# A relational graph network on one core: row fetches shared out over three engines, loops written out, weights kept

## What is computed

```python
def _rgcn_layer(x, src, dst, edge_type, W, W_root, b):
    out = x @ W_root + b
    x_src = x[src]
    for r in range(R):                       # R = 8
        mask = (edge_type == r).astype(x.dtype)
        agg = segment_sum(x_src * mask[:, None], dst, n)
        cnt = segment_sum(mask, dst, n)
        out = out + (agg / maximum(cnt, 1.0)[:, None]) @ W[r]
    return out

for i in range(3):
    h = _rgcn_layer(h, src, dst, edge_type, Ws[i], W_roots[i], bs[i])
    if i < 2: h = relu(h)
return layernorm(x + h)
```

## Time and profile before

| | us |
|---|---|
| device time, median of 3 runs | 3286.82 (3285.97 to 3287.74) |
| span of the profiled execution | 4636.9 |
| GpSimd busy in the span | 2366.0 |
| TensorE busy in the span | 2709.5 |
| VectorE busy in the span | 1593.4 |
| ScalarE busy in the span | 785.7 |

### The profile page before, as it was taken

One profiled execution on the slowest core, in us unless ns is written; L12 is line 12 of the kernel. 1 busy time (PEld: TensorE's weight loads), 2 busy tenths in 40 slices (PEclk: granted clock), 3 DMA queues, 4 the chain that ended last, 5 costly groups with the idle time before them and its releaser, 6 DMA issues. The chain is left out here.

```text
span 4636.9 us, 70372 instructions
## 1 busy us (share of the span) xinstructions
PE 2709.5 (58%) x16749; PEld 2382.2 (51%) x16750; DVE 1593.4 (34%) x7090; ACT 785.7 (17%) x1465; POOL 2366.0 (51%) x2511
## 2 busy tenths in 40 slices
PE   2676655656566723565666666661466566566567
PEld 1665545555555613555555555560455455555557
DVE  1343333333333512333333333360233333333336
ACT  1021111111111211111111111130111111111114
POOL 6125555555555064555555555507455555555540
PEclk5566677666667856767666666685666676766669
DMA  3001111111111021111111111113111111111110
GB/s 89 14 17 42 38 39 41 38 39 41 38 39 41 5 77 35 40 40 39 40 39 39 40 39 39 41 28 85 33 40 41 38 38 41 39 38 41 39 36 29
DMA packets 109300, 185.02 MB, mean 40 GB/s; under 512 B 41145, under 2 KB 66054, under 8 KB 109062
## 3 DMA queue, kind: packets, MB, share of 16 engines
q0 software_dynamic: 79872, 163.74, 13.5%
q1 hardware_dynamic: 29190, 19.05, 1.5%
HBM read 173.02 MB, written 9.60 MB: 39 GB/s over the span
## 5 line engine op out<-in xcount | busy, mean ns | idle before, releaser
L354 POOL DMA_INDIRECT ring<-node_table,idx x1664 | 1575.1, 947 | 1410.6 <-POOLq L229 969.9
L1018 PE MATMUL ps_o<-sums,w_rel 128*128 128x128 f32 x4992 | 1036.4, 393 | 501.6 <-PEq L229 501.6
L1008 PE MATMUL ps_a<-onehot,ring 128*128 128x128 f32 x4992 | 948.2, 350 | 558.3 <-PEq L229 290.1
L1018 PEld LDWEIGHTS ps_o<-sums,w_rel 128*128 128x128 f32 x4992 | 979.7, 301 | 552.6 <-issue 552.5
L354 POOL DMA_INDIRECT ring<-in_x,idx x832 | 788.5, 948 | 726.7 <-POOLq L229 509.4
L1008 PEld LDWEIGHTS ps_a<-onehot,ring 128*128 128x128 f32 x4992 | 821.2, 250 | 587.1 <-issue 580.9
L561 DVE TENSOR_SCALAR onehot<-iota,key,weight 128x128 f32<-128x128 f32 x2496 | 867.5, 360 | 309.4 <-issue 280.6
L786 ACT CAST oh_cell_t<-ps_r 64x512 bf16<-64x512 f32 x645 | 372.8, 578 | 1735.2 <-ACTq L229 1660.5
L797 ACT COPY sums<-ps_a 128x512 f32<-128x512 f32 x624 | 365.2, 585 | 1667.6 <-ACTq L229 1649.8
L451 DVE TENSOR_TENSOR oh_cell<-cell_t,iota_bf 128x256 bf16<-128x256 bf16 x663 | 194.4, 294 | 1272.0 <-DVEq L229 655.8
L987 PE MATMUL ps_w<-inv_parts,oh_cell_t 64*128 x2652 | 264.9, 173 | 487.3 <-issue 291.8
(11 more groups left out here) (144 smaller groups left out, 638.1 us busy)
## 6 DMA issues: line engine op xcount, KB each, us to landing
ring<-node_table,idx POOLq DMA_INDIRECT x1664
ring<-in_x,idx POOLq DMA_INDIRECT x832
node_table<-ring SPq DMA_DIRECT2D x24, 256.0 KB
out_rows<-ring SPq DMA_DIRECT2D x12, 256.0 KB
w_rel<-in_L_gnn_Ws SPq DMA_DIRECT2D x3, 512.0 KB
raw_dst<-in_dst SPq DMA_DIRECT2D x1, 384.0 KB
raw_src<-in_src SPq DMA_DIRECT2D x1, 384.0 KB
raw_typ<-in_edge_type SPq DMA_DIRECT2D x1, 384.0 KB
```

What stands on the lines that cost most here:

```text
L354: nc.gpsimd.indirect_dma_start(out=ring[:, q, t, :], out_offset=None, in_=source, in_offset=bass.IndirectOffsetOnAxis(ap=idx[:, q, t:t + 1 ...
L1008: ins = nc.tensor.matmul(ps_a[b][:, t * KEYS:(t + 1) * KEYS], ring[:, q, t, :], onehot[:, b, t, :], start=True, stop=True)
L1018: ins = nc.tensor.matmul(ps_o[b][:, 0:PAIR * WIN], w_rel[:, r, :], sums[:, b, r, :, :].rearrange("p t w -> p (t w)"), start=(r == 0), stop ...
```

## The change

- **Fetching.** 75 of the 2496 tiles are no longer fetched by GpSimd. SyncE fetches 15 tiles in each layer, the fourth of their quads: quads 2, 14, 27, 40, 53, 66, 79, 92, 104, 117, 130, 143, 156, 169, 182. ScalarE fetches 8 tiles in layer one (quads 26, 50, 75, 100, 125, 150, 175, 200) and 11 in the others (26, 43, 60, 78, 95, 113, 130, 147, 165, 182, 200), the third of their quads. Such a tile takes 128 DMAs of one row each, whose address comes from a register; a register load brings eight node numbers at a time. SyncE works through a tile in one go. ScalarE issues eight rows behind each quad's work, over 16 quads, starting 25 quads ahead. `sum_edges` waits on their semaphores too.
- **Weights.** They are looked up in layer one only (`look`), kept in `weight` by a maximum (`keep_weights`), and used again in layers two and three.
- **Loops.** All 208 quads of a layer are written out; columns have fixed addresses. `idx` and `refill` are gone: GpSimd reads node numbers from `src_t`, and ScalarE gives slots free (`ring_free`) in `evacuate`.
- **Start.** GpSimd waits for the number of passes before its first gather; that number is made earlier, ahead of `bkt_i` on VectorE. The staging tiles `f_*` no longer lie in the ring.

```diff
-NL = NT // (G * GT)
+NQ = NT // GT
+FREES = G // 2
+LOADS = 8
+SYNC_TILES = 15
+ACT_TILES = (8, 11)
...
 NPAD = N + WIN
+GROUPS = [-AHEAD + lo - LOOKS[3] for lo in LOOKS[3:-1]]
+GROUPS += [q for n in range(NQ // G + 1) for q in (n * G + lo for lo in LOOKS[:-1])]
+STARTS = [q + AHEAD for q in GROUPS if q + AHEAD < NQ]
+def spread(first, last, n):
+    return [first + (last - first) * k // max(n - 1, 1) for k in range(n)]
+def owners(kind):
+    sync = {q * GT + GT - 1: "sync" for q in spread(2, NQ - G, SYNC_TILES)}
+    act = {q * GT + GT - 2: "act" for q in spread(26, NQ - 8, ACT_TILES[kind])}
+    return {**sync, **act}
+OWNERS = [owners(kind) for kind in range(2)]
...
         picked = sb("picked", [P, G * GT, NEAR, PARTS], F32)
...
+            def row_numbers(tile, b):
+                sp.reg_add(idx_of[b], idx_of[b], 16)
+                sp.dma_start(row_idx[0:1, b, :], src[tile * P:(tile + 1) * P].rearrange("(o e) -> o e", o=1))\
+                  .then_inc(sync_idx_in[b], 16)
+            def gather_rows(source, kind):
+                tiles = [i for i in range(NT) if OWNERS[kind].get(i) == "sync"]
+                with sp.Fori(0, count_of):
+                    take(sp, sync_pass_open)
+                    row_numbers(tiles[0], 0)
+                    for n, tile in enumerate(tiles):
+                        b, q, t = n % 2, tile // GT % G, tile % GT
+                        if n + 1 < len(tiles):
+                            row_numbers(tiles[n + 1], (n + 1) % 2)
+                        rows_before, idx_now = sp.snap(rows_of[b]), sp.snap(idx_of[b])
+                        sp.reg_add(rows_of[b], rows_of[b], P * 16)
+                        if n >= 2:
+                            sp.wait_ge(sync_rows_in[b], rows_before)
+                        sp.wait_ge(sync_idx_in[b], idx_now)
+                        sp.sem_inc(sync_step, 1)
+                        take(sp, sync_step)
+                        if tile >= G * GT:
+                            take(sp, sync_slot_free)
+                        for e in range(0, P, LOADS):
+                            node = load_value(sp, row_idx[0:1, b, e:e + LOADS], 0, N - 1,
+                                              "the graph's edges join its nodes")
+                            for j in range(LOADS):
+                                sp.dma_start(ring[e + j:e + j + 1, q, t, :], source[bass.ds(node[j], 1), :])\
+                                  .then_inc(sync_rows_in[b], 16)
+                    rows_now = [sp.snap(reg) for reg in rows_of]
+                    for b in range(2):
+                        sp.wait_ge(sync_rows_in[b], rows_now[b])
+                    sp.sem_inc(sync_step, 1)
+                    take(sp, sync_step)
             load_weights(0, 48)
...
+                sp.sem_inc(table_ready_act, 1)
                 take(sp, w_used)
                 load_weights(layer, layer * 48 + 48)
+                gather_rows(table, 1)
             take(sp, h_free)
...
-
-                    take(pool, idx_full[q])
+            def gather(source, kind):
+                for q in range(NQ):
+                    take(pool, ring_free[q % FREES])
                     for t in range(GT):
+                        if q * GT + t in OWNERS[kind]:
+                            continue
                         nc.gpsimd.indirect_dma_start(
-                            out=ring[:, q, t, :], out_offset=None, in_=source,
-                            in_offset=bass.IndirectOffsetOnAxis(ap=idx[:, q, t:t + 1], axis=0))\
...
-                          .then_inc(gathered[q], 16)
-
-            gather_ring(x)
+                            out=ring[:, q % G, t, :], out_offset=None, in_=source,
+                            in_offset=bass.IndirectOffsetOnAxis(ap=src_t[:, q * GT + t:q * GT + t + 1], axis=0))\
+                          .then_inc(gathered[q % G], 16)
+            for q in range(G):
+                pool.sem_inc(ring_free[q % FREES], 1)
             take(pool, passes_ready[2])
             count_of = load_passes(pool)
-            more = load_value(pool, passes[0:1, 2:3], NL - 1, (BUCKETS + 1) * NL, "NL or more, less one")[0]
-            with pool.Fori(0, more):
-                gather_ring(x)
+            take(pool, src_cols_ready)
+            with pool.Fori(0, count_of):
+                gather(x, 0)
             with pool.Fori(1, L):
-
                 take(pool, table_ready)
                 with pool.Fori(0, count_of):
-                    with pool.Fori(0, NL):
-                        gather_ring(table)
+                    gather(table, 1)
         @block.vector
...
             dve.sem_inc(low_ready, 1)
+            take(dve, r_full_dve[0])
+            done(nc.vector.tensor_reduce(span_i[0:1, 0:1], ps_r[0][0:1, 0:P], AX.X, ALU.max))
+            dve.sem_inc(r_free[0], 1)
+            done(nc.vector.tensor_scalar(span_i[0:1, 1:2], span_i[0:1, 0:1], WIN.bit_length() - 1, None,
+                                         ALU.arith_shift_right))
+            done(nc.vector.tensor_scalar(passes[:, 0:1], span_i[0:1, 1:2], 1.0, None, ALU.add))
+            for s in passes_ready:
...
+            def next_windows(look):
                 nc.vector.tensor_scalar(base_k[:, :], base_k[:, :], float(WIN), float(N), ALU.add, ALU.min)
-                nc.vector.tensor_scalar(bucket_k[:, :], bucket_k[:, :], float(WIN // BN), float(BUCKETS),
-                                        ALU.add, ALU.min)
-                nc.vector.tensor_scalar(brel_k[:, :], brel_k[:, :], float(WIN // BN), None, ALU.subtract)
+                if look:
+                    nc.vector.tensor_scalar(bucket_k[:, :], bucket_k[:, :], float(WIN // BN), float(BUCKETS),
+                                            ALU.add, ALU.min)
...
+            def keep_weights(lo, hi):
+                take(dve, weights_step)
+                here = weight[:, lo * GT:hi * GT]
+                nc.vector.tensor_tensor(here, here, looked[:, 0:(hi - lo) * GT], ALU.max)\
+                    .then_inc(weights_step, 1)
...
-            def refill(first, q):
-
-
-                take(dve, oh_free[q % 2])
-                nc.vector.tensor_copy(idx[:, q, :], src_t[:, bass.ds(first + (G + q) * GT, GT)])\
-                  .then_inc(idx_full[q], 1)
...
-            def slot(first, q):
...
+            def slot(q, look):
+                group = None
+                if look:
+                    if q + AHEAD < NQ:
+                        cells(q + AHEAD)
+                    if q in GROUPS and GROUPS.index(q) - 2 < len(STARTS):
+                        group = GROUPS.index(q) - 2
+                        lo, hi, r = STARTS[group], (STARTS + [NQ])[group + 1], group % 2
...
                 for t in range(GT):
-                    if q + 2 < G:
-                        weigh(first, q + 2, t)
+                    if q + 2 < NQ:
+                        weigh(q + 2, t)
                     if q >= 2:
                         add_out(start, q - 2, t)
-                    if looks and t == 0:
-                        pick(r, tiles)
-                    if looks and t == 2:
-                        add_parts(at, r, tiles)
-                if looks:
+                    if group is not None:
+                        if t == 0:
+                            pick(r, (hi - lo) * GT)
+                        if t == 1:
+                            add_parts(r, (hi - lo) * GT)
+                        if t == 3:
+                            keep_weights(lo, hi)
+                if group is not None:
                     take(dve, weights_step)
                 if q >= 2 and q % 2 == 1:
...
-            def layer_sums():
+            def layer_sums(look):
                 with dve.Fori(0, count_of):
-                    dve.sem_inc(windows_full, 1)
+                    if look:
+                        dve.sem_inc(windows_full, 1)
                     keys()
-
-                    first_looked = (LOOKS[4] - LOOKS[3]) * GT
...
+                            cells(q)
+                            if q == hi + 1:
+                                which_bucket(lo, hi)
...
-                        for q in range(G + 2):
-                            slot(first, q)
+                    for q in range(2):
+                        take(dve, oh_free[q % 2])
+                        for t in range(GT):
+                            weigh(q, t)
+                    for q in range(NQ + 2):
+                        slot(q, look)
                     dve.wait_ge(added, 1)
                     for s in sums_ready:
                         dve.sem_inc(s, 1)
-
-                    for r in range(2):
-                        take(dve, weights_full[r])
-                        dve.sem_inc(weights_free[r], 1)
-                    take(dve, windows_free)
-                    next_windows()
+                    if look:
+                        take(dve, windows_free)
+                    next_windows(look)
             dve.sem_inc(added, 1)
             take(dve, first_ready)
```

(90 more changed lines are left out.)

231 lines of the change are left out of this document (120 added, 111 removed).

## The result

| | us | range of the runs |
|---|---|---|
| before | 3287.28 | 3285.97 to 3287.87 |
| changed | 3453.93 | 3443.64 to 3462.53 (4 runs) |
| ratio | 1.0508 | 95% interval 1.0495 to 1.0522 |

The change costs 167 us. The forecast was 3200 us, with a range up to 3430; the measured time lies above both, on the other side of "before".

A forecast was written before the change was run, and what follows sets the result against it. The prediction took GpSimd's gathers, 1.255 us each, to bound the kernel. Its terms 178 + 707 x 1.255 = 1065, + 30 + 1011.5 + 30 + 1011.5 + 47.6 gave 3196 us, forecast as 3200, range 3170 to 3430.

The forecast's parts named there:

- That GpSimd's gathers set the time of before: Kernel before, without recording: GpSimd's gather spacing binds all three layers, 2392 x 1.255 = 3002 us of the time.
- the sum from 1.255 us a gather: Kernel before: gathers at 1.255 us plus what they don't cover, 175 + 914 + 31 + 1044 + 31 + 1044 + 48 = 3287 us.
- The forecast's case: Whole changed kernel: GpSimd still binds, a SyncE tile takes at most 62 us; 3196 us by the sum, chance 0.54.
- The loops at nothing: GpSimd's 24 loop ends, written out: taken as 0, between 30 us gained and 20 us lost.
- the sums without look-ups at nothing: Layers two and three: less work for TensorE and VectorE a quad gains nothing by itself, as it lies beside the gathers.
- D = 61.6 us: SyncE's time for one tile of 128 rows: 128 x 0.42 + 16 x 0.43 + 1, bounds 43 and 75 us.
- 16 x 0.43: SyncE's register loads in a tile: 16 loads of eight node numbers, 0.39 us each, 0.43 with the gap.
- The limit, and the price above it: SyncE's tile time may reach 61.8 us in layers two and three, 63.3 in layer one; each us above both costs 45.
- ScalarE's 4.1 us a quad: ScalarE's eight rows, a load and waits behind a quad, in 176 of 208 quads: 4.1 us, below GpSimd's 4.86.
- let SyncE run through from 25 us on: Layer one: SyncE begins at about 25 us, so the layer needs 118 us plus 15 tile times, against GpSimd's 1068.
- SyncE binds: Rival: TensorE waits for SyncE's last tiles, GpSimd for slots; at 67 us a tile 3407 us, chance 0.22.
- The two hinder each other: Rival: SyncE's and ScalarE's DMA issues exclude each other, a SyncE tile takes 69.7 us, the time 3529 us; chance 0.13.

The follow-up runs named there:

- a kernel in which SyncE was quick: The changed kernel, with node numbers loaded once a SyncE tile and the same eight used for all 128 rows (wrong rows, for time alone): 3196.71 us.
- fifteen late: The changed kernel with its 15 SyncE tiles a layer spread from quad 2 to 200 in place of 182: 3265.91 us, ratio 0.9931.

## Why the prediction was wrong

**That GpSimd's gathers set the time of before: right, for a wrong reason.** The step took the span of 4636.9 us for an effect of the recording, and with it the idle time of TensorE during the gathers. It was neither: in the second recording of the same kernel both are gone. What held is the sum from 1.255 us a gather. A layer takes 1071.6 us in the kernel before (2198.78 - 1127.21 in the new recording) and 1069.4 without row copies (2198.04 - 1128.61), against 1075 by the sum. The gain is 34 us for 30 gathers, and 86 us for 67 (13 SyncE tiles and 30 on ScalarE, less two in the first ring fill that count nothing; 67 x 1.255 = 84). The forecast's case gave 3196; a kernel in which SyncE was quick took 3196.7. That the sum for the kernel before fits to 1 us was luck, as the prediction says: GpSimd gets its first freed slot at 184.1 us, not 175, and shorter layers and a shorter end make up for it.

**The loops at nothing, the sums without look-ups at nothing: right.** Ratio 0.9998 [0.9988, 1.0007]. They aren't idle, though: ScalarE's eleven tiles fit into layers two and three, where the look-ups are gone, and cost 31 us for three of them in layer one, where they aren't.

**D = 61.6 us: this step failed, in one term.** "16 x 0.43" for the loads of node numbers was 16 x 0.85. The rows were right: 0.411 us against 0.42. Term by term: 61.6 + 16 x 0.42 - 128 x 0.009 + 0.2 = 67.4. The 0.43 came from loads of one and of four values, read on GpSimd's and VectorE's queues (0.30 to 0.40 and 0.34 us), as if size and engine hardly mattered. On SyncE four values take 0.557 us. The trace of before held a warning: ScalarE's load of a single value took 0.47 us, more than VectorE's of four.

```profile
L232 ACTq TENSOR_LOAD <-passes x1: 472/472/472, 280.6 to 280.6; - x1
```

The forecast's text itself named "loads of eight values over 0.6 us" as a sign of being wrong, yet gave the load no bounds of its own apart from those of D.

**The limit, and the price above it: right.** By its formula D = 67.4 costs (67.4 - 61.8) x 30 + (67.4 - 63.3) x 15 = 230 us, so 3196 + 230 = 3426. A layer took 1125.6 us. The sum has 87 + 15 x 67.4 and 27 for the change of layer (the 30 less the 3 in them for the last gather to land), 1125 us.

**ScalarE's 4.1 us a quad: 0.3 too low, without effect here.** In layer two of the changed kernel its copies of `sums` start at 1502.62, 1506.88 and 1511.36 us, 4.3 and 4.5 us apart, under GpSimd's 4.86. The load was mis-sized here too (0.72 us against 0.39), but ScalarE had the room.

**Layer one: a wait was missed, 25 us.** The step let SyncE run through from 25 us on. But its third tile (quad 27) needs the slot of quad 1, which becomes free only after the counting, once that quad has been summed:

```profile
96.25 65.88 SPq L369 DMA_DIRECT2D ring<-in_x  x128
162.28 0.23 SPq L343 DMA_DIRECT2D row_idx<-in_src  x1
190.10 10.13 SPq L369 DMA_DIRECT2D ring<-in_x  x21
```

SyncE waits from 162.5 to 190.1 us. That it waits for the slot is shown by the runs in which the third tile lies elsewhere: in quads 29, 30 and 32 (fourteen tiles, fifteen late, thirteen) it starts at 199.2, 205.3 and 212.9 us. The other 13 tiles begin at 190.1 us: 190.1 + 13 x 67.4 = 1066 us, where its last row is issued at 1068. The early start of 25 us was worth two tiles, no more. This wait is most of the rest between 3426 and 3453.9 us. So this step failed too: with the load alone mis-sized the time would have been near 3426 us, inside the range.

**The rivals.** "SyncE binds" (0.22) is what happened, with the mechanism as told: TensorE waits for SyncE's tiles, and GpSimd stands. Its place was right and its size (D = 67, 3407 us) nearly so; what it named as its cause, slower DMAs and gaps, was not the cause. "The two hinder each other" (0.13) fell: 0.225 us a DMA on SyncE with and without ScalarE's, and 0.213 us on ScalarE beside it. So what the Trainium skill says in "Perfetto Trace Analysis", section "DMA Instruction — HWDGE (DVE, Sync)", of a descriptor generator locked for exclusive use did not show here at 0.41 us a row on one queue and eight rows in 4.4 us on the other, not even where the two overlapped (0.230 against 0.229 us).

**The range.** A sum that stands 0.2 us from a limit, with 45 us behind every us, is no forecast of one side. The bounds of D were 43 and 75 us, yet 0.54 went to a value below 62 that hung on a load that no row showed. 16 x 0.42 us of that load made the kernel slower and not faster. In the account of what the range leaves out, the 0.03 for times below 3170 is also part of chances that already add up to 1 without it.

## What to carry to other kernels

A helper engine's work has to be priced by rows of its own kind, on its own queue: same operation, same number of values. Where none exists, size the helper's share so that the highest bound still fits, since a tile too few costs 1.3 us a layer, and the fifteenth cost 63 (3265 to 3454 us over three layers). When work in fixed order is handed to a helper, count also the slot that it waits for at the start, and what stands behind its last piece: the same 15 tiles cost 3454 us or 3266 by their places alone.

## What the runs showed of the hardware that had not been expected

- A TENSOR_LOAD (register load) of eight values takes 0.78 us on SyncE and 0.72 on ScalarE, one of four 0.557 us on SyncE and 0.343 on VectorE.
- Of the 0.411 us between two single-row copies the DMA itself is 0.225 us. Without an address step for every row, rows come 0.33 us apart (128 in 42.35 us).
- Single-row DMAs issued by SyncE while one of ScalarE's was under way took 0.230 us on average, those that overlapped none 0.229.
- One recorded execution of the kernel before took 4636.9 us, another 3285.9, and the timed runs 3286 to 3288.
